# A channel-mixing stage whose two partition halves hold odd and even image rows instead of the same rows

## The chip, the cores and the metric

The kernel runs on one core of a Trainium2 chip. The metric is the device time of one execution in microseconds (us). All data are float32. Five engines work side by side and meet at semaphores: TensorE (PE in the profile; its weight loads are PEld), VectorE (DVE), ScalarE (ACT), GpSimd (POOL) and SyncE (SP), which only issues DMAs here. ScalarE and GpSimd issue DMAs too. A name such as ACTq or SPq is the engine's sequencer.

## The reference

The input x is 8 images x 64 channels x 256 x 256 pixels. Two layers are applied; only the first is touched by the change:

```python
x = x + _L0_conv_ref(_gn(x), ...)      # layer 0: the stage of this document
x = x + _L1_conv_ref(_gn(x), ...)      # layer 1: FFT, 32x32 modes mixed, inverse FFT
# inside _L0_conv_ref
y  = einsum('bwhc,dc->bwhd', xp, mlp1_w) + mlp1_b
x1 = _shift1(y[..., :c]);  x2 = _shift2(y[..., c:2*c])   # quarter of the channels each: one pixel
x3 = sigmoid(xn * wbn) * x                               # up, down, left, right, edges repeated
out = bar[:, 0] * x1 + bar[:, 1] * x2
o = (einsum('bwhc,dc->bwhd', out, mlp2_w) + mlp2_b) * x3
```

Since the shifts, the two products with matrices and the factors of `bar` are linear, an output pixel of layer 0 is a sum over four neighbours (above, below, left, right) of a 64x64 matrix by the 64 channels of that neighbour, plus a constant, times a gate `sigmoid(...)`, plus 1, times the centred input pixel.

## The kernel before

The program runs in stages, each ended by a barrier of all engines: statistics of x (0 to about 338 us), a short serial computation of the matrices and scales (to about 388 us), **the mixing stage** (to about 1471 us), the second normalisation, the forward transforms, the mixing of modes, and the inverse transforms. The change touches the end of the serial computation and the mixing stage.

The mixing stage handles 128 tiles: 8 images x 16 tiles of 16 image rows. They are numbered n = 0 to 31 in a body that runs 4 times (two images in each). There are 4 buffers of each kind (`mix_x`, `centred`, `gated`), 2 of `mix_out`, and two halves of PSUM. TensorE contracts over 128 partitions, twice the 64 channels, so two neighbours are summed in one pass. The lower 64 partitions hold an image row one column to the right of where the upper 64 hold it, and the upper ones hold the row one further down. Half of a tile's rows come by DMA into the lower partitions and half into the upper ones; VectorE copies each half to the other partitions. What each tile takes:

- SyncE (L565, L568): two loads of 9 rows x 64 channels, 576 KB each, when the tile four before has been convolved and gated.
- VectorE: copy `up` (L687) when both loads have landed; copy `down` (L692).
- GpSimd (L590, `pad`): two small products that repeat the edge columns, after `down`. They signal `padded`.
- TensorE (L618): 16 matrix products of 64 output channels x 512 pixels, after `padded`. A float32 product is two passes, so the trace has 32 records.
- ScalarE: centring of the pixel values (L641; two instructions of 64 partitions on even tiles, one on odd tiles, whose other half VectorE centres in L700), then the sigmoid (L649). It waits for `padded` too.
- VectorE: gate times convolution (L722, out of PSUM), later the output (L731).
- ScalarE: the store of the output (L662, 1024 KB), and the sum of its squares (L667).

The order on VectorE for tile n is: up(n+2), L722 of n, down(n+2), L731 of n, centre(n+2) if odd. On ScalarE: centring and sigmoid of n+2, store of n, square of n. Nothing reorders instructions within an engine.

The matrices stand in `wall`, 128 columns for each image: two slots of 64, for rows held in the lower and the upper partitions. At L503 32 instructions scale them out of PSUM. `take` (L677 to L679) fetches one image's matrices for the stage.

Of the kernel before, what the change touches and what calls it, by code (L numbers as in the profile page):

```python
# [23 lines left out]
ACT = mybir.ActivationFunctionType  # L24
ALU = mybir.AluOpType
# [19 lines left out]
LAYOUT = ((0, 0, 2), (1, 0, 1), (0, 1, 0), (1, 1, 3))  # L45
PITCH = W + 1
# [67 lines left out]
def program(nc, x, w1m, b1m, w2m, b2m, sa1, sa2, gamma, beta, wr1, wi1, wr2, wi2, const, out):  # L114
    top = ExitStack()
    with top:
# [34 lines left out]
        wall = sb(top, "wall", [P, B + 1, P])  # L151
# [7 lines left out]
        with ph:  # L159
# [133 lines left out]
            with nc.Block() as block:  # L293
# [77 lines left out]
                def _(dve):  # L371
# [141 lines left out]
        with ph:  # L513
            NX = 4
            XT = [sb(ph, f"mix_x{i}", [P, MR + 1, PITCH]) for i in range(NX)]
# [4 lines left out]
            one = sb(ph, "one", [P, MR + 1])  # L520
            wcur = [sb(ph, f"wcur{i}", [P, P]) for i in range(2)]
            pcur = [sb(ph, f"pcur{i}", [P, 6]) for i in range(2)]
            loaded = [sem(f"mix_loaded{i}") for i in range(NX)]
            stored = [sem(f"mix_stored{i}") for i in range(2)]
            one_set = sem("mix_one_set")
            doubled, padded, batch_ready = sem("mix_doubled"), sem("mix_padded"), sem("mix_batch_ready")
# [4 lines left out]
            ITER = B // 2  # L531

            x1_par = x1.rearrange("b (r e) c w -> b (e c) r w", e=2)

            def split(n):

                return n % 2 == 1

            def loaded_by(i, n):

                q, t = n % NX, n % NB
                edge = 16 if q in (0, NX - 1) else 0
                batch = NB // NX * 32 + edge
                return i * (2 * batch) + n // NB * batch + (t // NX + 1) * 32 + (edge if q == 0 or t == NB - 1 else 0)

# [6 lines left out]
            with nc.Block() as block:  # L552
                @block.sync
                def _(sp):
                    with sp.Fori(0, ITER) as i:
                        for n in range(NI):
                            ch = bass.ds((i * 2 + n // NB) * C, C)
                            t, xt = n % NB, XT[n % NX]


                            sp.wait_ge(conv_done, i * NI + n + 1)
                            sp.wait_ge(sig_done, i * NI + n + 1)
                            r0 = t * MR - 1
                            lo = max(r0, 0)
                            sp.dma_start(xt[0:C, lo - r0:MR // 2 + 1, 1:W + 1],  # L565
                                         x_rows[ch, lo:r0 + MR // 2 + 1, :]).then_inc(loaded[n % NX], 16)
                            hi = min(r0 + MR + 2, H)
                            sp.dma_start(xt[C:P, MR // 2:hi - r0 - 1, 0:W],  # L568
                                         x_rows[ch, r0 + 1 + MR // 2:hi, :]).then_inc(loaded[n % NX], 16)

                            if t == 0:
                                sp.dma_start(xt[0:C, 0:1, 1:W + 1], x_rows[ch, 0:1, :]).then_inc(loaded[n % NX], 16)
                            if t == NB - 1:
                                sp.dma_start(xt[C:P, MR:MR + 1, 0:W], x_rows[ch, H - 1:H, :]
                                             ).then_inc(loaded[n % NX], 16)

# [4 lines left out]
                def _(pool):  # L581
# [12 lines left out]
                    pad(0, 0)  # L594
                    pad(0, 1)

                    def body(i, final):
                        for n in range(NI - 2 * final):
                            pad(i, n + 2)

                    iterations(pool, body)

                @block.tensor
                def _(pe):
                    pe.sem_inc(conv_done, NX)
                    with pe.Fori(0, ITER) as i:
                        for n in range(NI):
                            j, k = n // NB, n % 2
# [13 lines left out]
                            last.then_inc(conv_done, 1)  # L622

                @block.scalar
                def _(act):
# [5 lines left out]
                    def gate(i, n):  # L631
# [7 lines left out]
                        for half in range(1 if split(n) else 2):  # L639
                            h = slice(half * C, (half + 1) * C)  # L640
                            last = nc.scalar.activation(  # L641
                                XC[n % NX][h, :].rearrange("p (r w) -> p r w", w=W),
# [710 lines left out]
```

## Time and profile before

| | us |
|---|---|
| device time, median of 3 runs (3144.79 to 3153.17) | 3149.35 |
| device time of the profiled execution | 3155.57 |
| span of the profiled execution | 3153.8 |
| mixing stage, first VectorE copy to last output | 397.2 to 1471.0 |
| VectorE busy in 430 to 1470 us | 966.1 of 1040 |
| TensorE busy there | 909.8 |
| ScalarE busy there | 865.6 |

The span runs from the first to the last instruction; the device time has 1.8 us more around it. Busy shares over the whole span (TensorE 71%, VectorE 64%) mix stages with different limits, so the mixing stage is read by itself. "Idle before" in the profile is the idle time of the engine just ahead of an instruction, with what ended it; "issue" means that nothing the profile shows was waited for. TensorE's granted clock was 0.96 of full speed in 430 to 1470 us.

### The profile page before, as it was taken

The page shows a single profiled execution, that of the slowest core. Times are in us where ns is not written, and L with a number is a line of the kernel's source. Part 1 is how long each engine was busy: PE and PEld are TensorE (multiplying, and loading weights), DVE is VectorE, ACT ScalarE, POOL GpSimd, SP SyncE. Part 2 cuts the span into 40 slices and gives each one's busy share as a digit, 9 for nine tenths or more (in the row PEclk, how much of TensorE's full clock was granted, in tenths as well). Part 3 has the DMA queues.
Part 4 walks back from the last instruction along what each step waited for, and adds up shares of the span by engine and source line. Part 5 has one row for each costly group of instructions (what it writes and reads, how often), then busy time and mean ns, then how long its engine had stood idle before and what let it go on. Part 6 is the DMA issues. An engine that isn't in the chain of part 4 may idle for free. (4 is left out here: it accounts for less than half of the span.)

```text
span 3153.8 us, 39097 instructions
## 1 busy us (share of the span) xinstructions
PE 2252.6 (71%) x12960; PEld 1081.7 (34%) x12960; DVE 2027.7 (64%) x2317; ACT 1298.2 (41%) x1470; POOL 756.3 (24%) x477
## 2 busy tenths in 40 slices
PE   0000289888989888885999999945554898988784
PEld 0000123223323232331455444425553444444442
DVE  8999689989999999996665565620000454544442
ACT  1111078878887888885332232310000222212220
POOL 1000022332233322332655455500000111111112
PEclk9999999999999999998999999977787999998987
DMA  9999199999999999997877666669998999999999
GB/s 400 429 429 429 36 248 265 271 248 275 270 272 256 270 274 270 269 267 233 316 261 266 241 242 247 232 145 295 304 305 231 384 401 380 394 380 408 389 378 351
DMA packets 537808, 942.87 MB, mean 299 GB/s; under 512 B 16896, under 2 KB 459952, under 8 KB 493136
## 3 DMA queue, kind: packets, MB, share of 16 engines
q1 hardware_dynamic: 299264, 613.33, 61.9%
q10 hardware_dynamic: 202880, 192.95, 20.1%
q0 software_dynamic: 35536, 134.84, 11.2%
q8 instruction: 85, 1.39, 0.2%
q14 instruction: 43, 0.35, 0.0%
HBM read 647.46 MB, written 293.60 MB: 298 GB/s over the span
## 5 line engine op out<-in xcount | busy, mean ns | idle before, releaser
L618 PE MATMUL psum<-mix_x,wcur 128*64 128x512 f32 x4096 | 937.6, 614 | 150.3 <-POOL mix_x L590 134.3
L618 PEld LDWEIGHTS psum<-mix_x,wcur 128*64 128x64 f32 x4096 | 316.6, 139 | 770.8 <-issue 566.4
L1259 PE MATMUL psum<-tab_irow_icol_sign,inv_t 128*128 128x512 f32 x1024 | 495.8, 608 | 18.9 <-DVE inv_x L1306 16.0
L590 POOL TENSOR_TENSOR mix_x<-mix_x,one 64x17 f32<-64x17 f32 x256 | 323.2, 1262 | 747.6 <-DVE mix_x L692 740.2
L641 ACT ACTIVATE centred<-mix_x,pcur 64x2048 f32<-64x2048 f32 x192 | 384.2, 2001 | 204.1 <-POOL mix_x L590 188.9
L1077 POOL TENSOR_TENSOR fwd_diff<-x_tile 128x2048 f32<-128x2048 f32 x64 | 307.9, 4812 | 291.7 <-PE psum L869 256.5
L983 ACT ACTIVATE fwd_rows<-psum 128x512 f32<-128x512 f32 x256 | 152.2, 597 | 412.8 <-PE psum L869 387.9
L263 DVE BATCH_NORM_STATS2 stats<-stat_x 128x512 f32 x512 | 310.0, 678 | 17.5 <-DMA stat_x<-x 14.7
L731 DVE SCALAR_TENSOR_TENSOR mix_out<-gated,centred 128x2048 f32<-128x2048 f32 x128 | 293.6, 2294 | 41.3 <-issue 35.5
L722 DVE SCALAR_TENSOR_TENSOR gated<-psum,pcur,gated 128x2048 f32<-128x2048 f32 x128 | 300.9, 2351 | 16.3 <-PE psum L618 14.4
L1052 DVE COPY fwd_cols<-psum 128x136 f32<-128x136 f32 x512 | 154.6, 394 | 234.2 <-PE psum L880 233.2
L869 PE MATMUL psum<-fwd_sum,tab_ident_frow_fcol 128*64 128x512 f32 x512 | 282.3, 635 | 30.1 <-POOL fwd_diff L1077 20.3
L1287 ACT ACTIVATE inv_t<-psum 128x256 f32<-128x256 f32 x256 | 98.1, 383 | 478.5 <-PE psum L1250 478.5
L1122 PE MATMUL psum<-mode_w,mode_x 128*16 128x64 f32 x4096 | 169.9, 360 | 162.5 <-DMA mode_x<-modes_in 159.8
L869 PE MATMUL psum<-fwd_diff,tab_ident_frow_fcol 128*64 128x512 f32 x512 | 282.7, 636 | 0.0
L649 ACT ACTIVATE gated<-centred,pcur 128x2048 f32<-128x2048 f32 x128 | 268.2, 2095 | 13.3 <-DVE centred L700 5.1
L1306 DVE TENSOR_TENSOR inv_x<-inv_x,psum 128x1024 f32<-128x1024 f32 x128 | 155.6, 1220 | 176.0 <-PE psum L1259 142.0
L1306 DVE TENSOR_TENSOR x_tile<-x_tile,psum 128x1024 f32<-128x1024 f32 x128 | 156.0, 1221 | 168.1 <-PE psum L1259 159.5
L1259 PEld LDWEIGHTS psum<-tab_irow_icol_sign,inv_t 128*128 128x128 f32 x1024 | 199.0, 196 | 167.6 <-issue 149.1
L297 PE MATMUL psum<-s_ones_dmask_spread_npix,w1d 128*64 128x128 f32 x1 | 0.4, 396 | 342.1 <-PEq L200 342.1
L667 ACT ACTIVATE square<-mix_out 128x2048 f32<-128x2048 f32 x128 | 242.5, 1894 | 3.6 <-DVE mix_out L731 3.6
L1250 PE MATMUL psum<-tab_irow_icol_sign,inv_yy 128*128 128x256 f32 x512 | 159.1, 395 | 100.6 <-ACT inv_yy L1281 100.6
(183 smaller groups left out, 1952.5 us busy)
## 6 DMA issues: line engine op xcount, KB each, us to landing
x_tile<-x_scratch SPq DMA_DIRECT2D x184, 1024.0 KB, 7.7
mix_x<-x SPq DMA_DIRECT2D x240, 576.0 KB, 8.2
stat_x<-x SPq DMA_DIRECT2D x64, 2048.0 KB, 14.4
x_scratch<-mix_out ACTq DMA_DIRECT2D x128, 1024.0 KB, 9.1
inv_x<-x_scratch SPq DMA_DIRECT2D x64, 1024.0 KB, 10.9
out<-x_tile POOLq DMA_DIRECT2D x64, 1024.0 KB, 17.0
out<-inv_x POOLq DMA_DIRECT2D x64, 1024.0 KB, 15.6
mode_w<-L_conv_w_imag ACTq DMA_DIRECT2D x16, 2048.0 KB, 21.2
```

The lines of the kernel that those rows point to most:

```text
L263: last = nc.vector.bn_stats(stats[:, bass.ds(b * (NT * 48) + (t * 8 + q) * 6, 6)], XT[t % NX][:, q * 512:(q + 1) * 512])
L590: last = nc.gpsimd.tensor_tensor(XT[n % NX][h, :, to], XT[n % NX][h, :, of], one[h, :], ALU.mult)
L618: last = nc.tensor.matmul(bank(k * 4 + q, 512, C, par * C), wcur[j][:, m * C:(m + 1) * C], XT[n % NX][:, r0:r0 + 3:2, m:m + W], start=(m = ...
L641: last = nc.scalar.activation(XC[n % NX][h, :].rearrange("p (r w) -> p r w", w=W), XT[n % NX][h, 1:MR:2, 1 - half:1 - half + W], ACT.Ident ...
L649: nc.scalar.activation(G[n % NX][:, :], XC[n % NX][:, :], ACT.Sigmoid, bias=pcur[j][:, 1:2], scale=pcur[j][:, 0:1]).then_inc(sig_done, 1)
L667: nc.scalar.activation(SQ[:, :], XO[k][:, :], ACT.Square, accum_out=sqs[:, bass.ds(i * NI + n, 1)]).then_inc(sq_done, 1)
L722: nc.vector.scalar_tensor_tensor(out=G[n % NX][:, :], in0=psum[:, k * SC:(k + 1) * SC], scalar=pcur[j][:, 3:4], in1=G[n % NX][:, :], op0=A ...
L731: nc.vector.scalar_tensor_tensor(out=XO[k][:, :], in0=G[n % NX][:, :], scalar=1.0, in1=XC[n % NX][:, :], op0=ALU.add, op1=ALU.mult, accum_ ...
L869: last = nc.tensor.matmul(bank(n % 2, 512, C, par * C), frow[:, par, :], ED[G0 % 2][par][:, 2 * cp:2 * cp + 2, :], start=True, stop=True)
L1077: nc.gpsimd.tensor_tensor(ED[G0 % 2][1][:, :, :], XW[G0 % NX][:, 0, :, :], XW[G0 % NX][:, 1, :, :], ALU.subtract).then_inc(diff_done, 1)
L1259: last = nc.tensor.matmul(bank(n % 2 * 2 + a), TS[n % 2][:, a * P:(a + 1) * P], icol, start=True, stop=True)
L1306: nc.vector.tensor_tensor(xw, xw, psum[:, n % 2 * 1024:n % 2 * 1024 + 1024] .rearrange("p (a k) -> p a k", a=2), ALU.add).then_inc(added, 1)
```

## The change

The two partition halves no longer hold the same rows. Odd image rows go to the lower 64 partitions, one column to the right, and even rows to the upper 64. A second set of buffers, `mix_a`, holds the same rows the other way aligned: VectorE copies each half within its own partitions. Of the 16 products of a tile the first eight (m = 0) read `mix_x` and the last eight (m = 1) read `mix_a`. Since neighbours swap their roles between even and odd output rows, there are four matrix slots of 64 columns for each image instead of two, and `LAYOUT` has eight entries; the scaling is one product per entry over all eight images.

Besides: the loads stay 9 rows x 64 channels each, but take every other row (1 KB each). Even rows are loaded from SyncE's queue, odd rows from ScalarE's, behind the store. `pad` waits for the loads alone, not for the copies, and has four products; ScalarE's centring waits for the loads alone; TensorE waits for `copied` only ahead of m = 1. VectorE centres in tiles 1 and 5 of every 8 instead of in every odd tile. `A_LOADED` is empty, so its branches add nothing.

```diff
-LAYOUT = ((0, 0, 2), (1, 0, 1), (0, 1, 0), (1, 1, 3))
-PITCH = W + 1
+LAYOUT = ((0, 0, 0), (1, 0, 3), (0, 1, 2), (1, 1, 1),
+          (0, 2, 1), (1, 2, 2), (0, 3, 3), (1, 3, 0))
...
-                    for b in range(B):
-                        for half, slot, d in LAYOUT:
-                            h = slice(half * C, (half + 1) * C)
-                            v.tensor_scalar(wall[h, b, slot * C:(slot + 1) * C], mats[h, b, d, :],
-                                            sm[h, 6, b:b + 1], None, ALU.mult)
+                    for half, slot, d in LAYOUT:
+                        h = slice(half * C, (half + 1) * C)
+                        v.tensor_tensor(wall[h, 0:B, slot * C:(slot + 1) * C], mats[h, :, d, :],
+                                        sm[h, 6, :].unsqueeze(2).to_broadcast([C, B, C]), ALU.mult)
...
-            XT = [sb(ph, f"mix_x{i}", [P, MR + 1, PITCH]) for i in range(NX)]
+            NK = TR // 2
+            XT = [sb(ph, f"mix_x{i}", [P, NK + 1, W + 2]) for i in range(NX)]
+            XA = [sb(ph, f"mix_a{i}", [P, NK, W + 1]) for i in range(NX)]
...
+            ODD, EVEN = slice(0, C), slice(C, P)
+            A_LOADED = ()
+            CENTRE_DVE = (1, 5)
...
+                            sp.wait_ge(conv_done, i * NI + n + 1)
+                            sp.wait_ge(sig_done, i * NI + n + 1)
+                            count = NK + (t != NB - 1)
+                            last = min(t * TR + 2 * NK, H - 2)
+                            sp.dma_start(xt[EVEN, 0:count, 0:W],
+                                         x_rows[ch, t * TR:last + 1:2, :]).then_inc(loaded[q], 16)
...
-                        pool.wait_ge(doubled, i * NI + n + 1)
-                        for half, to, of in ((0, 0, 1), (1, W, W - 1)):
-                            h = slice(half * C, (half + 1) * C)
-                            last = nc.gpsimd.tensor_tensor(XT[n % NX][h, :, to], XT[n % NX][h, :, of],
-                                                           one[h, :], ALU.mult)
+                        xt, xa = XT[n % NX], XA[n % NX]
+                        pool.wait_ge(loaded[n % NX], loaded_by(i, n))
...
+                        for h, to, of in ((ODD, xt[ODD, :, 0], xt[ODD, :, 1]),
+                                          (EVEN, xt[EVEN, :, W], xt[EVEN, :, W - 1]),
+                                          (ODD, xa[ODD, :, W], xt[ODD, 1:NK + 1, W]),
+                                          (EVEN, xa[EVEN, :, 0], xt[EVEN, 0:NK, 0])):
+                            last = nc.gpsimd.tensor_tensor(to, of, one[h, 0:to.shape[1]], ALU.mult)
                         last.then_inc(padded, 1)
...
                             for m in range(2):
-                                for q in range(4):
+                                if m == 1 and not a_by_dma(n):
+                                    pe.wait_ge(copied, i * len(COPIES) + copies_before(n) + 1)
+                                for q in range(NK // 2):
                                     for par in range(2):
-                                        r0 = 1 - m + par + q * 4
+                                        if m == 0:
+                                            src = xt[:, 2 * q + par:2 * q + par + 2, 1 - par:1 - par + W]
+                                        else:
+                                            src = xa[:, 2 * q:2 * q + 2, par:par + W]
                                         last = nc.tensor.matmul(bank(k * 4 + q, 512, C, par * C),
-                                                                wcur[j][:, m * C:(m + 1) * C],
-                                                                XT[n % NX][:, r0:r0 + 3:2, m:m + W],
-                                                                start=(m == 0), stop=(m == 1))
+                                                                wcur[j][:, (2 * m + par) * C:(2 * m + par + 1) * C],
+                                                                src, start=(m == 0), stop=(m == 1))
...
-                        act.wait_ge(padded, i * NI + n + 1)
+                        act.wait_ge(loaded[n % NX], loaded_by(i, n))
...
+                    def load_odd(i, n):
...
+                        act.dma_start(xt[ODD, int(t == 0):NK + 1, 1:W + 1],
+                                      x_rows[ch, r0:t * TR + TR:2, :]).then_inc(loaded[q], 16)
...
+                    for n in range(NX):
+                        load_odd(0, n)
...
+                            if not (final and n + NX >= NI):
+                                act.wait_ge(conv_done, i * NI + n + NX + 1)
+                                act.wait_ge(sig_done, i * NI + n + NX + 1)
+                                load_odd(i + (n + NX) // NI, (n + NX) % NI)
...
+                    def first(i, n):
 
                         dve.wait_ge(loaded[n % NX], loaded_by(i, n))
...
+                        if not a_by_dma(n):
+                            nc.vector.tensor_copy(XA[n % NX][ODD, :, 0:W], XT[n % NX][ODD, 1:NK + 1, 1:W + 1])
+
+                    def second(n):
+
+                        if not a_by_dma(n):
+                            nc.vector.tensor_copy(XA[n % NX][EVEN, :, 1:W + 1], XT[n % NX][EVEN, 0:NK, 0:W]
+                                                  ).then_inc(copied, 1)
```

On ScalarE, from the start of the repeated body, the store of tile n (`x_scratch<-mix_out`) stood between the sigmoid of n+2 and the square of n. Before:

```order
L641 ACTIVATE centred<-mix_x,pcur 64x2048 x2
L649 ACTIVATE gated<-centred,pcur 128x2048
L661 REGISTER_ALU
L662 ISA
L662 DMA x_scratch<-mix_out 128x8x256
L666 REGISTER_ALU
L667 ISA
L667 ACTIVATE square,sqs<-mix_out 128x2048
L636 REGISTER_ALU
L641 ACTIVATE centred<-mix_x,pcur 64x2048
```

The same place in the changed kernel:

```order
L680 ACTIVATE centred<-mix_x,pcur 64x2048 x2
L686 ACTIVATE gated<-centred,pcur 128x2048
L710 REGISTER_ALU
L711 ISA
L711 DMA x_scratch<-mix_out 128x8x256
L694 ISA
L694 DMA mix_x<-x 64x9x256
L720 REGISTER_ALU
L721 ISA
L721 ACTIVATE square,sqs<-mix_out 128x2048
L675 ISA
L677 REGISTER_ALU
```

The load of the odd rows (L694, for tile n+4) now stands behind the store on ScalarE and its queue, ahead of the square; the next tile's centring has two instructions there, where it had one.

On VectorE, one tile after the first of the body. Before (L687 is `up`, L692 `down`, L700 the centring of the tile two on):

```order
L687 COPY mix_x<-mix_x 64x8x256
L720 REGISTER_ALU
L722 SCALAR_TENSOR_TENSOR gated<-psum,pcur,gated 128x2048
L692 COPY mix_x<-mix_x 64x8x256
L728 REGISTER_ALU
L730 REGISTER_ALU
L731 ISA
L731 SCALAR_TENSOR_TENSOR mix_out,sums<-gated,centred 128x2048
L700 TENSOR_SCALAR centred<-mix_x,pcur 64x2048
L685 REGISTER_ALU
```

In the changed kernel the same tile:

```order
L745 COPY mix_a<-mix_x 64x8x256
L768 REGISTER_ALU
L770 SCALAR_TENSOR_TENSOR gated<-psum,pcur,gated 128x2048
L750 COPY mix_a<-mix_x 64x8x256
L776 REGISTER_ALU
L778 REGISTER_ALU
L779 ISA
L779 SCALAR_TENSOR_TENSOR mix_out,sums<-gated,centred 128x2048
L739 REGISTER_ALU
```

The two copies stay where they were, and the centring behind the output is gone from this tile.

## Rows read from the trace of the kernel before

**Rows 1.** Windows: width, busy us (count) of PE PEld DVE ACT POOL, clock, DMA, GB/s.

```profile
core 0: us, PE busy (x) PEld busy (x) DVE busy (x) ACT busy (x) POOL busy (x), PEclk, DMA share, GB/s
100.00:300.00 200.00, 0.00 (x0) 0.00 (x0) 197.90 (x327) 30.98 (x174) 0.00 (x0) 1.00 1.01 428
393.00:408.00 15.00, 7.60 (x26) 2.42 (x28) 6.24 (x5) 7.52 (x5) 1.79 (x4) 0.60 1.13 202
430.00:1470.00 1040.00, 909.80 (x3982) 307.57 (x3978) 966.12 (x709) 865.55 (x563) 314.22 (x248) 0.96 1.04 266
1014.70:1016.20 1.50, 1.50 (x8) 0.41 (x6) 1.49 (x2) 1.39 (x2) 0.00 (x0) 1.00 1.09 386
1018.00:1021.50 3.50, 3.14 (x16) 0.85 (x12) 3.35 (x6) 2.13 (x4) 2.56 (x2) 1.00 1.12 205
```

**Rows 2.** Waits, 430 to 1470 us: who <- for whom: us, times, longest.

```profile
POOL mix_x L590 <- DVE mix_x L692: 712.1, 124, 17.0
ACT centred L641 <- POOL mix_x L590: 143.9, 59, 10.6
PE psum L618 <- POOL mix_x L590: 110.4, 72, 5.7
DVE mix_out L731 <- issue: 35.5, 41, 2.0
DVE gated L722 <- PE psum L618: 14.4, 11, 4.8
```

**Rows 3.** Groups by line, 430 to 1470 us: count, busy us, mean ns, idle before.

```profile
L641 ACT ACTIVATE centred<-mix_x,pcur 64x2048 f32<-64x2048 f32 x186 | 372.2, 2001 | 159.1 <-POOL mix_x L590 143.9 <-issue 14.4
L590 POOL TENSOR_TENSOR mix_x<-mix_x,one 64x17 f32<-64x17 f32 x248 | 314.2, 1267 | 719.3 <-DVE mix_x L692 712.1
L722 DVE SCALAR_TENSOR_TENSOR gated<-psum,pcur,gated 128x2048 f32<-128x2048 f32 x125 | 293.9, 2351 | 16.2 <-PE psum L618 14.4
L731 DVE SCALAR_TENSOR_TENSOR mix_out<-gated,centred 128x2048 f32<-128x2048 f32 x126 | 289.0, 2294 | 41.2 <-issue 35.5 <-DMA x_scratch<-mix_out 3.1
L649 ACT ACTIVATE gated<-centred,pcur 128x2048 f32<-128x2048 f32 x125 | 261.9, 2095 | 13.2 <-DVE centred L700 5.1 <-ACT centred L641 0.8
L692 DVE COPY mix_x<-mix_x 64x2048 f32<-64x2048 f32 x124 | 151.8, 1224 | 3.9
L700 DVE TENSOR_SCALAR centred<-mix_x,pcur 64x2048 f32<-64x2048 f32 x62 | 79.8, 1287 | 2.0
```

**Rows 4.** DMA issues: count, KB each, us to landing; 430:1470, then 388:400 us.

```profile
mix_x<-x SPq DMA_DIRECT2D x227, 576.0 KB, 8.1
x_scratch<-mix_out ACTq DMA_DIRECT2D x125, 1024.0 KB, 9.1
...
mix_x<-x SPq DMA_DIRECT2D x1, 512.0 KB, 5.4
```

**Rows 5.** DMA queues, 1024.5 to 1026 us: packets, MB, share of 16 engines.

```profile
q1 hardware_dynamic: 261, 0.27, 55.5%
q10 hardware_dynamic: 295, 0.29, 55.3%
```

**Rows 6.** Timeline, 1007 to 1028 us: start, us, what [idle before].

```profile
1007.54 0.60 SPq L568 DMA_DIRECT2D mix_x<-x  x1
...
1009.37 0.38 ACTq L662 DMA_DIRECT2D x_scratch<-mix_out  x1
...
1014.03 7.11 PE L618 MATMUL psum<-mix_x,wcur 128*64 128x512 f32 x32 [0.56 <-POOL mix_x L590]
...
1026.42 0.51 POOL L590 TENSOR_TENSOR mix_x<-mix_x,one 64x17 f32<-64x17 f32 x2 [4.97 <-DVE mix_x L692]
...
1027.34 2.29 DVE L731 SCALAR_TENSOR_TENSOR mix_out<-gated,centred 128x2048 f32<-128x2048 f32 x1 [1.00 <-issue]
```

**Rows 7.** Timeline of the serial computation before the stage, 366 to 388 us.

```profile
366.93 0.69 DVE L487 TENSOR_TENSOR w2s<-psum,w2t 128x512 f32<-128x512 f32 x1
...
378.37 9.52 DVE L503 TENSOR_SCALAR wall<-psum,sm 64x64 f32<-64x64 f32 x32 [6.82 <-PE psum L353]
```

More of the change, by code:

```diff
@@ L150, in program @@
         params = sb(top, "params", [P, B + 1, 4])
-        wall = sb(top, "wall", [P, B + 1, P])
+        wall = sb(top, "wall", [P, B + 1, 4 * C])
         sums = sb(top, "sums", [P, B * NT])
@@ L519, in program @@
             SQ = sb(ph, "square", [P, SC])
-            one = sb(ph, "one", [P, MR + 1])
-            wcur = [sb(ph, f"wcur{i}", [P, P]) for i in range(2)]
+            one = sb(ph, "one", [P, NK + 1])
+            wcur = [sb(ph, f"wcur{i}", [P, 4 * C]) for i in range(2)]
             pcur = [sb(ph, f"pcur{i}", [P, 6]) for i in range(2)]
             loaded = [sem(f"mix_loaded{i}") for i in range(NX)]
+            a_loaded = [sem(f"mix_a_loaded{i}") for i in range(NX)]
             stored = [sem(f"mix_stored{i}") for i in range(2)]
             one_set = sem("mix_one_set")
-            doubled, padded, batch_ready = sem("mix_doubled"), sem("mix_padded"), sem("mix_batch_ready")
+            copied, padded, batch_ready = sem("mix_copied"), sem("mix_padded"), sem("mix_batch_ready")
             xc_done, sig_done, conv_done, sq_done = (sem("mix_" + n) for n in ("xc", "sig", "conv", "sq"))
@@ L531, in program, with a_by_dma, centre_dve, copies_before @@
             ITER = B // 2
-            x1_par = x1.rearrange("b (r e) c w -> b (e c) r w", e=2)
-            def split(n):
-                return n % 2 == 1
+            ODD, EVEN = slice(0, C), slice(C, P)
+            A_LOADED = ()
+            CENTRE_DVE = (1, 5)
+            COPIES = [n for n in range(NI) if n % 8 not in A_LOADED]
+            CENTRES = [n for n in range(NI) if n % 8 in CENTRE_DVE]
+            x1_par = x1.rearrange("b (r e) c w -> b (e c) r w", e=2)
+            def a_by_dma(n):
+                return n % 8 in A_LOADED
+            def centre_dve(n):
+                return n % 8 in CENTRE_DVE
+            def copies_before(n):
+                return sum(m < n for m in COPIES)
+            def centres_before(n):
+                return sum(m < n for m in CENTRES)
             def loaded_by(i, n):
@@ L544, in loaded_by, with a_loaded_by, row_pair @@
                 return i * (2 * batch) + n // NB * batch + (t // NX + 1) * 32 + (edge if q == 0 or t == NB - 1 else 0)
+            def a_loaded_by(i, n):
+                mine = [m for m in range(NI) if a_by_dma(m) and m % NX == n % NX]
+                return i * (len(mine) * NK * 16) + (mine.index(n) + 1) * NK * 16
+            def row_pair(first, step):
+                return bass.AP(x.tensor, first, [[C * NPIX, B], [step, 2], [NPIX, C], [1, W + 1]])
             def iterations(engine, body):
@@ L554, in _, with load @@
                 def _(sp):
+                    def load(i, n):
+                            bs = bass.ds(i * 2 + n // NB, 1) if not isinstance(i, int) else slice(i * 2 + n // NB, i * 2 + n // NB + 1)
+                            ch = bass.ds((i * 2 + n // NB) * C, C) if not isinstance(i, int) else slice((i * 2 + n // NB) * C, (i * 2 + n // NB + 1) * C)
+                            t, xt, xa, q = n % NB, XT[n % NX], XA[n % NX], n % NX
+                            sp.wait_ge(conv_done, i * NI + n + 1)
[4 more added lines that the diff above has]
+                                         x_rows[ch, t * TR:last + 1:2, :]).then_inc(loaded[q], 16)
+                            if t == NB - 1:
+                                sp.dma_start(xt[EVEN, NK, 0:W], x_rows[ch, H - 1, :]).then_inc(loaded[q], 16)
+                            if a_by_dma(n):
+                                for k in range(NK):
+                                    sp.dma_start(xa[:, k, :],
+                                                 row_pair((t * TR + 2 * k + 1) * W, -W - 1)[bs][0]
+                                                 ).then_inc(a_loaded[q], 16)
@@ L555, in _ @@
                     with sp.Fori(0, ITER) as i:
                         for n in range(NI):
[L557 to L575, printed above, removed]
+                            load(i, n)
@@ L585, in pad @@
                     def pad(i, n):
[L587 to L601 removed]
+                        xt, xa = XT[n % NX], XA[n % NX]
+                        pool.wait_ge(loaded[n % NX], loaded_by(i, n))
+                        if a_by_dma(n):
+                            pool.wait_ge(a_loaded[n % NX], a_loaded_by(i, n))
+                        for h, to, of in ((ODD, xt[ODD, :, 0], xt[ODD, :, 1]),
[3 more added lines that the diff above has]
+                            last = nc.gpsimd.tensor_tensor(to, of, one[h, 0:to.shape[1]], ALU.mult)
+                        last.then_inc(padded, 1)
+                    with pool.Fori(0, ITER) as i:
+                        for n in range(NI):
+                            pad(i, n)
                 @block.tensor
@@ L708, in _ @@
                     for n in range(2):
-                        up(0, n)
-                        down(n)
-                    centre(0, 1)
+                        first(0, n)
+                        second(n)
                     def body(i, final):
@@ L717, in body @@
                             if ahead:
-                                up(i, n + 2)
+                                first(i, n + 2)
                             dve.wait_ge(conv_done, i * NI + NX + n + 1)
@@ L725, in body @@
                             if ahead:
-                                down(n + 2)
+                                second(n + 2)
                             dve.wait_ge(h_done, i * NI + 2 + n + 1)
@@ L735, in body @@
                                                            ).then_inc(o_done, 1)
-                            if ahead and split(n + 2):
-                                centre(i, n + 2)
                             if n % NB == NB // 2:
```

41 lines of the change are left out of this document (20 added, 21 removed).

## The prediction, made before the changed kernel was run

> **What bounds the kernel now.** I read the windows first, then the waits, the groups by line, and the DMA views, all of the mixing stage. In 430 to 1470 us VectorE has 125 instructions of L722, one for each tile, so a tile takes 1040/125 = 8.32 us. Per tile VectorE is busy 966.1/125 = 7.73 us, TensorE 7.28, ScalarE 6.92 [rows 1, 3]. VectorE is the nearest to a bound, with 0.59 us of idle time a tile. The waits say where it comes from: 35.5 us ahead of L731 for nothing that the profile names, 14.4 us for TensorE [rows 2]; the remaining 24 us are short gaps, 0.19 us a tile. The 35.5 us belong to GpSimd: in the timeline the pair of pads runs from 1026.42 for 0.51 us, and L731, which should follow the copy, starts at 1027.34 after 1.00 us idle [rows 6]. When the pads lose that race they take long instead: 1.27 us each on average, over 0.25 in the pair shown [rows 3, 6]. TensorE and ScalarE wait for the pads, 110 and 144 us [rows 2]: pads wait for the copy `down`, which stands behind L722 of two tiles before. So VectorE, GpSimd and TensorE form a ring in which nobody runs ahead.
>
> The DMA engines are the second bound. Per tile they carry two loads of 576 KB and a store of 1024 KB, 2.23 MB, which at 8.32 us is 268 GB/s, as the window has it (266). When loads alone run they make 202 to 205 GB/s; a store alone makes 386, and the statistics stage, whose loads fill all 128 partitions, 428 [rows 1]. So a load into 64 partitions goes at half rate. One after the other a tile's transfers would take 1.18/0.203 = 5.8 us and 1.05/0.386 = 2.7, together 8.5 us, more than the tile. They fit only because a store and a load overlap at their ends: in 1.5 us queue q10 (stores) moved 0.29 MB and q1 (loads) 0.27, 180 GB/s for the load as if it were alone [rows 5]. No engine waits for it, though; only the latency of a load would show.
>
> **The change part by part.**
>
> *Matrices.* 32 scalings at L503 take 9.52 us in a row; now 8 products of 64x512 out of PSUM. The nearest row is the 128x512 product out of PSUM, 0.69 us [rows 7]. 8 x 0.69 = 5.5, a gain of 4.0 us on a serial path. Bounds: 0.4 each (gain 6) and 1.0 each (gain 1.5).
>
> *VectorE.* Copies stay, 64x2048 at 1.22 us each. The centring falls from 1 in 2 tiles to 1 in 4: 0.25 x 1.29 = 0.32 us a tile less. Busy 7.73 - 0.32 = 7.41, with short gaps 0.19 it is 7.60. The L722 waits for TensorE (0.12 a tile) go, see below. `take` copies 256 columns instead of 128, once in 16 tiles: nothing.
>
> *Pads.* Four instead of two, 9 and 8 elements instead of 17, started by the loads and not by the copy. By the mean of 1.27 us they take 5.1 us a tile instead of 2.5, between 1.0 (0.25 each, unhindered) and 9.5 (2.4 each, one VectorE instruction each); below the tile's time but for the last. VectorE pays now 0.28 us a tile for the race (35.5/125). It could be 0 if the pads fall under L722, or 1.0 if every tile loses as the one shown. I keep 0.28, as the row has it: 7.60 + 0.28 = 7.88.
>
> *ScalarE.* 0.25 x 2.00 = 0.50 more a tile, 6.92 + 0.50 = 7.42, and it no longer waits for the pads. It issues the load of odd rows, 0.60 us as SyncE does, behind the store's 0.38 [rows 6]. Behind these waits the square; the sigmoid (2.10 us) runs meanwhile and hides both if the output is done by then. Uncovered they cost up to 1.0, which makes 8.4; I take 0.2 and 7.6.
>
> *TensorE.* The same 16 products, 7.11 us [rows 6]. They start on the pads, which no longer hang on L722. Tile n+1 can start when L722 of n-1 has read its half of PSUM, and `copied` comes 1.2 us after that, well ahead of m = 1. TensorE gets ahead by most of a tile. This takes the 110 us of waits off the ring.
>
> *Loads.* Same bytes (9 + 9 rows before and after), every other row. Even rows for n+5 are issued about 1.4 us into L722 of n (2.35 + 7.11 less one tile); nobody needs them for a tile and a half. Odd rows for n+4 are issued only when the output of n is done. VectorE needs them at `first` of n+4, right behind the output of n+1. That closes a new ring over two tiles: output done, signal and store issue 0.58; the load's latency L; then first 1.22 and its share of centring 0.32, L722 2.35, second 1.22, output 2.37, gaps 0.2. Twice the tile's time is at least 8.25 + L. For L: the first load of the stage landed 5.4 us after its issue with 512 KB [rows 4], of which 2.6 is data at 202 GB/s, so 2.8 are fixed. Behind the store: 2.8 + 2.7 (store) + 2.9 (own data) - 0.5 (store issued earlier) = 7.9 us. The ring then is (8.25 + 7.9)/2 = 8.08 us. Bounds of L: 5.0 if the even rows and the store cost it nothing, 10.3 if the even load of n+6, whose data starts 0.5 us into it, takes half the engines and adds the remaining 2.4.
>
> *A rule against it.* The Trainium skill (SBUF — State Buffer, "Can I just issue two DMAs to hit both halves?") says that two DMAs at once, one at partition 0 and one at 64, came out only 6% faster than one: they serialise. The windows of loads, 202 and 205 GB/s, agree for two DMAs of one queue; rows 5 shows a load and a store of two queues side by side, 371 GB/s. By the rule a tile's transfers would stay at 5.5 + 2.7 = 8.2 us, by the row they could fall to about 5.8.
>
> *Sum.* VectorE with the pads gives 7.88, the load ring 8.08, ScalarE 7.6. I take 8.10, at which the DMA moves 275 GB/s. (8.32 - 8.10) x 128 = 28 us. Matrices 4.0. The start of the stage: the loads of the first tiles ran at 202 GB/s; on two queues they may land earlier, by 0 to 5 us; I take 1. The profiled execution took 3155.6: 3155.6 - 33 = 3122.6. It stood 6.2 above the median of the runs, so 3116 us.
>
> **The rivals.**
>
> *B, both halves load side by side.* If odd and even rows on two queues use different sides of the memory, the loads of a tile cost nearly the time of one. L falls towards 6 and VectorE with its pads binds: 7.88, and 7.8 if it wins the race more often. (8.32 - 7.85) x 128 = 60, with 4 and 4 for the start: 3149 - 68 = 3081. For: rows 5. Against: 202 GB/s for pairs of loads, and the rule above.
>
> *C, the freed time is taken back.* Twice as many pads, now started while VectorE is anywhere, cost it 0.7 us a tile instead of 0.28: 7.60 + 0.7 = 8.3, and only the matrices are gained: 3145. For: each of the 41 waits cost 0.87 us (35.5/41). Against: under L722 no wait of VectorE shows.
>
> *D, slower: the odd rows come late.* One mechanism: the odd load waits behind the 1 MB store, and shares the engines with the next even load. VectorE then waits at `first` (L739) in each tile. It decides from L = 2 x 8.32 - 8.25 = 8.4 us, 0.5 above my estimate. With L = 9.1 the tile is 8.68 and the kernel takes 3149 + 46 - 5 = 3190; with 10.3 it is 9.28: +123 - 5 = 3267. For: stores land after 9.1 us at the median now, and this load stands behind one [rows 4]. Against: the store's 9.1 contains the two loads issued just ahead of it (the second at 1007.54, the store at 1009.37 [rows 6]); now the even load is issued some 5 us earlier. The Trainium skill (DMA: Bandwidth & Descriptors, "Queues, rings and completion order") has each DMA engine take turns between queues, which is what would slow the odd load; rows 5 shows such turns, without a loss for the load.
>
> **How the numbers follow.** Forecast 0.42, its own range 3098 to 3138; B 0.18; C 0.14; D 0.26. Likeliest 3116. The range for 8 in 10 is 3070 to 3200: it takes in B and C, and the part of D up to L = 9.3, about half of it; outside are 0.13 of D and 0.03 below. 0.3% of 3149 is 9.4 us, about what the measurement can tell from no change. Faster: forecast and B, 0.60. Same: C, 0.14. Slower: D, 0.26.
>
> **What would show it.** The scaling of the matrices near 5.5 us. In the stage: TensorE without waits for pads but with waits for L770; ScalarE busy about 7.4 us a tile; the centring on VectorE at 32 instructions. The ring of loads right: VectorE waits a little for `mix_x<-x` at L745 or L742, odd loads land after some 8 us. B: loads above 300 GB/s while no store runs, and no waits for DMA. C: idle time ahead of L779, L745 or L750 for "issue". D: long waits of VectorE for DMA, odd loads landing after more than 8.5 us. The prediction is wrong in its core if the tile takes under 7.85 or over 8.4 us, or if ScalarE turns out to be what the others wait for.

## The result, and the profile after

The changed kernel takes 3206.4 us (median of 4 runs, 3202.35 to 3217.43); the kernel before 3151.3 beside it. The ratio is 1.017, 95% interval 1.015 to 1.019: slower by 1.7%, clear of the noise. The forecast was 3116. The profiled execution took 3217.4 us, 61.8 over that of before. From the first load to the last output the mixing stage went from 1082.4 to 1145.5 us, +63.1; the matrices gave 4.0 back; what follows the stage took 2.7 more. So the whole loss lies in the stage. L770 to L770 a tile takes 8.90 us on the mean of tiles 8 to 120; for before the same count gives 8.35.

The stage's window for the changed kernel, columns as in [rows 1]:

```profile
430.00:1520.00 1090.00, 912.49 (x3934) 329.43 (x3932) 902.30 (x669) 924.47 (x583) 274.46 (x491) 0.95 1.04 250
```

VectorE was busy 93% of the stage before, now 83% (902.3 of 1090). ScalarE is at 85%. The DMA moves 250 GB/s instead of 266. No engine is at a bound. That is the picture of a ring: a circle of waits in which each step needs the one before it, so the time round it decides, not the work of one engine. The waits of the changed kernel in this stretch, as in [rows 2]:

```profile
POOL mix_x L624 <- DMA mix_x<-x: 789.8, 122, 10.0
PE psum L651 <- DVE gated L770: 160.5, 79, 5.8
ACT square L721 <- issue: 131.9, 36, 5.8
DVE mix_a L745 <- DMA mix_x<-x: 106.8, 63, 4.5
DVE centred L742 <- DMA mix_x<-x: 73.2, 31, 5.0
```

VectorE now waits 180 us for loads, at the first thing that it does for a tile; in [rows 2] there was no such wait. TensorE no longer waits for the pads but for VectorE to free PSUM. ScalarE's 131.9 us "issue" ahead of the square are, by the order of its program, its wait for the output, with store and load issued behind it. The waits in [rows 2] ahead of L731, 35.5 us, are gone: L779 now has 3.8.

```profile
L680 ACT ACTIVATE centred<-mix_x,pcur 64x2048 f32<-64x2048 f32 x215 | 430.2, 2001 | 17.0 <-issue 11.4 <-DMA mix_x<-x 1.4
L770 DVE SCALAR_TENSOR_TENSOR gated<-psum,pcur,gated 128x2048 f32<-128x2048 f32 x123 | 287.2, 2335 | 0.0
L779 DVE SCALAR_TENSOR_TENSOR mix_out<-gated,centred 128x2048 f32<-128x2048 f32 x123 | 282.1, 2293 | 3.8
L624 POOL TENSOR_TENSOR mix_x<-mix_x,one 64x9 f32<-64x9 f32 x245 | 188.4, 769 | 797.0 <-DMA mix_x<-x 789.8
```

The instructions last what they lasted in [rows 3], but the pads are shorter: 0.77 us here and 0.35 for the two on `mix_a`, not 1.27. The DMA view, as in [rows 4]:

```profile
x_scratch<-mix_out ACTq DMA_DIRECT2D x122, 1024.0 KB, 6.5
mix_x<-x ACTq DMA_DIRECT2D x115, 576.0 KB, 8.8
mix_x<-x SPq DMA_DIRECT2D x112, 576.0 KB, 8.3
```

And two tiles in the timeline, start and duration, with the idle time before:

```profile
1000.46 2.29 DVE L779 SCALAR_TENSOR_TENSOR mix_out<-gated,centred 128x2048 f32<-128x2048 f32 x1
...
1003.03 2.10 ACT L686 ACTIVATE gated<-centred,pcur 128x2048 f32<-128x2048 f32 x1
1003.25 0.39 ACTq L711 DMA_DIRECT2D x_scratch<-mix_out  x1
1003.86 0.62 ACTq L694 DMA_DIRECT2D mix_x<-x  x1
...
1013.64 1.22 DVE L745 COPY mix_a<-mix_x 64x2048 f32<-64x2048 f32 x1
1013.69 1.51 POOL L624 TENSOR_TENSOR mix_x<-mix_x,one 64x9 f32<-64x9 f32 x2 [5.65 <-DMA mix_x<-x]
...
1018.41 2.29 DVE L779 SCALAR_TENSOR_TENSOR mix_out<-gated,centred 128x2048 f32<-128x2048 f32 x1
```

The output of a tile ends at 1002.75. ScalarE is still centring for another tile, dispatches its sigmoid at 1003.03, and issues store and odd load at 1003.25 and 1003.86. The load lands 9.8 us later, at 1013.62, and the copy of that tile starts at 1013.64. The output that follows two tiles on ends at 1020.7: 18 us for two tiles.

### The profile page after: what moved, and what is told of

It is laid out like the page before. It is cut to its first block and busy times, and to the rows that moved or that the text cites. A ratio compares the mean times of both kernels' runs of the same rounds, so it can differ in the third digit from the quotient of the medians.

```text
span 3215.5 us, 39423 instructions
## 1 busy us (share of the span) xinstructions
PE 2271.3 (71%) x12960; PEld 1108.6 (34%) x12960; DVE 1971.2 (61%) x2261; ACT 1374.5 (43%) x1502; POOL 719.1 (22%) x733
## 5 line engine op out<-in xcount | busy, mean ns | idle before, releaser
L651 PE MATMUL psum<-mix_x,wcur 128*64 128x512 f32 x2048 | 516.5, 645 | 194.9 <-DVE gated L770 160.5
L651 PE MATMUL psum<-mix_a,wcur 128*64 128x512 f32 x2048 | 471.4, 596 | 0.0
L680 ACT ACTIVATE centred<-mix_x,pcur 64x2048 f32<-64x2048 f32 x224 | 448.2, 2001 | 48.1 <-DMA mix_x<-x 32.4
L624 POOL TENSOR_TENSOR mix_x<-mix_x,one 64x9 f32<-64x9 f32 x256 | 194.5, 760 | 830.9 <-DMA mix_x<-x 823.4
L651 PEld LDWEIGHTS psum<-mix_x,wcur 128*64 128x64 f32 x2048 | 171.7, 146 | 528.4 <-issue 510.3
L721 ACT ACTIVATE square<-mix_out 128x2048 f32<-128x2048 f32 x128 | 243.5, 1903 | 149.6 <-issue 131.9
L770 DVE SCALAR_TENSOR_TENSOR gated<-psum,pcur,gated 128x2048 f32<-128x2048 f32 x128 | 299.0, 2336 | 1.9 <-PE psum L651 1.9
L779 DVE SCALAR_TENSOR_TENSOR mix_out<-gated,centred 128x2048 f32<-128x2048 f32 x128 | 293.5, 2293 | 4.0
L651 PEld LDWEIGHTS psum<-mix_a,wcur 128*64 128x64 f32 x2048 | 171.9, 137 | 275.4 <-issue 274.8
```

The costliest lines, as they stand in the source:

```text
L624: last = nc.gpsimd.tensor_tensor(to, of, one[h, 0:to.shape[1]], ALU.mult)
L651: last = nc.tensor.matmul(bank(k * 4 + q, 512, C, par * C), wcur[j][:, (2 * m + par) * C:(2 * m + par + 1) * C], src, start=(m == 0), stop ...
L680: last = nc.scalar.activation(out, rows, ACT.Identity, bias=pcur[j][(EVEN, ODD)[half], 4:5])
L721: nc.scalar.activation(SQ[:, :], XO[k][:, :], ACT.Square, accum_out=sqs[:, bass.ds(i * NI + n, 1)]).then_inc(sq_done, 1)
L770: nc.vector.scalar_tensor_tensor(out=G[n % NX][:, :], in0=psum[:, k * SC:(k + 1) * SC], scalar=pcur[j][:, 3:4], in1=G[n % NX][:, :], op0=A ...
L779: nc.vector.scalar_tensor_tensor(out=XO[k][:, :], in0=G[n % NX][:, :], scalar=1.0, in1=XC[n % NX][:, :], op0=ALU.add, op1=ALU.mult, accum_ ...
```

## The experiments

The ring theory: the odd load for tile n+4 leaves after the output of n and its store, and VectorE needs it right behind the output of n+1. Its work from there ends with the output of n+2, two tiles after the start of the circle. So two tiles cannot take less than the way round. Rival S: ScalarE has too much work, since it centres in three tiles of four. Rival R: every other row loads more slowly. The runs were made in three groups, e1 to e4, e5 to e8, e9 and e10, each with runs of the kernel before beside it; where times of different groups are subtracted below, the ratios to the kernel before give the same within 7 us.

For each kernel the way round was read from the trace (means of tiles 8 to 119, us). The four parts always add up to two tiles, so the sum alone shows no ring; the ring binds where the third, from landing to the copy, is small. It holds a few hundredths for the signal and VectorE's centring, 1.3 us in one tile of four. In the changed kernel VectorE starts on a tile within 0.15 us of the landing in 85 of 112 tiles, in e2 in 60, in e3 in 72, in e1 in none.

| kernel | output done to issue | issue to landing | landing to first copy | first copy to output n+2 | tile |
|---|---|---|---|---|---|
| before (upper load) | -7.29 | 9.28 | 7.06 | 7.65 | 8.35 |
| changed | 1.09 | 8.94 | 0.64 | 7.14 | 8.90 |
| e1, all on SyncE | -9.47 | 10.30 | 7.02 | 7.34 | 7.60 |
| e2, odd load before output | 0.47 | 7.23 | 0.78 | 7.14 | 7.81 |
| e3, load ahead of store | 1.31 | 6.75 | 0.64 | 7.15 | 7.92 |
| e4, before, split queues | 4.73 | 8.36 | 0.08 | 7.25 | 10.21 |
| e5, centring in odd tiles | 0.95 | 8.67 | 0.87 | 7.14 | 8.82 |
| e10, first copy later | 1.28 | 9.73 | 0.89 | 4.86 | 8.38 |

**e1: all loads on SyncE.**

```diff
 # SyncE, behind the even rows of the same tile
+                            sp.dma_start(xt[ODD, int(t == 0):NK + 1, 1:W + 1],
+                                         x_rows[ch, r0:t * TR + TR:2, :]).then_inc(loaded[q], 16)
 # ScalarE
-                    for n in range(NX):
-                        load_odd(0, n)
...
-                                load_odd(i + (n + NX) // NI, (n + NX) % NI)
```

> The changed kernel with one edit: the odd rows are loaded by SyncE right behind the even rows of the same tile (both when the tile four before is convolved and gated), and ScalarE issues only stores. Ring theory (the odd load is issued only after the output of tile n, behind the store, and VectorE needs it at the output of n+1): the ring is gone, VectorE no longer waits for mix_x<-x, a tile takes 8.0 to 8.2 us instead of 8.90, and the kernel 3095 to 3130 us, faster than before. Rival S (ScalarE has too much work since it centres in three tiles of four, and TensorE and VectorE follow it): a tile stays over 8.5 us, 3165 us or more, and the idle time of VectorE moves to a wait for ScalarE. Rival R (rows read every other one are slower to load): loads alone run under 190 GB/s and VectorE still waits for them, 3180 or more.

Measured: 3058.3 us, ratio to before 0.970 (0.967 to 0.972). That is 148 us under the changed kernel. VectorE waits for no load any more. Window and waits of this kernel:

```profile
430.00:1370.00 940.00, 873.18 (x3950) 320.20 (x3946) 902.05 (x673) 923.62 (x588) 182.74 (x488) 0.99 1.08 292
```

```profile
PE psum L656 <- DVE gated L768: 49.5, 40, 2.8
DVE mix_out L777 <- issue: 21.4, 25, 2.4
```

Direction and mechanism are as the ring theory had it, but the gain is larger than expected: 7.60 us a tile, not 8.0 to 8.2, and 3058 us, not 3095 to 3130. ScalarE is busy 98% here, VectorE 96%. Rivals S and R fall as causes of the slowdown: ScalarE does the same centring and the rows are the same ones.

**e2: odd load on ScalarE, ahead of the wait for the output.** The block with `load_odd` moves up, with its own waits (left out here):

```diff
+                                load_odd(i + (n + NX) // NI, (n + NX) % NI)
                             act.wait_ge(o_done, i * NI + NX + n + 1)
                             act.dma_start(x1_par[...], XO[k]...)
```

> The changed kernel with the odd load still on ScalarE's queue, but issued ahead of the wait for the output of tile n, so ahead of that tile's store too. Ring theory: the load leaves 3 to 6 us earlier and has no store ahead of it, VectorE stops waiting for it, 8.0 to 8.2 us a tile, within 10 us of the kernel with all loads on SyncE. Rival S: no gain, 3165 or more. If only the sharing of the DMA engines by two queues delayed the load, it would still land late, after 8.5 us, and the gain would be under half.

Measured: 3077.5 us, 0.976 (0.974 to 0.979), 7.81 us a tile: 19 us over e1, where at most 10 were expected, and faster than the 8.0 to 8.2 us a tile named. The detail was a miss too. The load still leaves 0.47 us after the output on the mean, not 3 to 6 us earlier, since ScalarE is then just done with the centring of n+2; only the store is out of its way, and VectorE still waits for loads, 44 us in all:

```profile
DVE centred L742 <- DMA mix_x<-x: 23.1, 29, 1.5
DVE mix_a L745 <- DMA mix_x<-x: 21.0, 29, 2.0
```

The two queues are still there, and 129 of the 148 us are back. So it is not two queues in themselves that cost the time.

**e3: the load ahead of the store, both after the output.**

```diff
                             act.wait_ge(o_done, i * NI + NX + n + 1)
+                                load_odd(i + (n + NX) // NI, (n + NX) % NI)
                             act.dma_start(x1_par[...], XO[k]...)
```

> The changed kernel with the order of the two DMAs on ScalarE swapped: after the output of tile n first the odd load of n+4, then the store of n. Ring theory with the store's 2.7 us of data as part of the latency: the load's latency falls from 8.9 to about 6.2 us and its issue comes 0.6 earlier, the ring asks only for (17.8 - 3.3)/2 = 7.3 us and no longer binds; 8.0 to 8.3 us a tile, 3100 to 3145. If the latency is not the store's, but that of the even load sharing the engines, it stays near 8 and the tile near 8.5 us, 3155 or more.

Measured: 3092.6 us, 0.981 (0.979 to 0.984). The latency falls from 8.94 to 6.75 us, by 2.2 us. The time is 7 us under the range named (3100 to 3145), and 7.92 us a tile is under its 8.0 to 8.3. The argument was too kind all the same: the latency is not 6.2, the issue after the output is not earlier (1.31), and the ring still binds in most tiles, with 52 us of VectorE's waits (28.8 at L744, 23.1 at L741).

**e4: the queue part alone, in the kernel before.**

```diff
-                            sp.dma_start(xt[C:P, MR // 2:hi - r0 - 1, 0:W],
+                        act.dma_start(xt[C:P, MR // 2:hi - r0 - 1, 0:W],   # behind the store of tile n
                                       x_rows[ch, r0 + 1 + MR // 2:hi, :]).then_inc(loaded[n % NX], 16)
```

> The kernel before with the queue part of the change alone: the load of the upper partitions goes from SyncE to ScalarE, behind the store of tile n. Ring theory: the same ring arises, and it is longer, since here the store is issued 4.2 us after the output (ScalarE waits for the pads): 4.9 + 8.9 + 7.6 = 21.4 us for two tiles, 10.7 a tile at most, and if ScalarE gets ahead in the slower kernel down to 8.9; 3220 to 3450 us, clearly slower than before, with VectorE waiting for mix_x<-x. If two queues in themselves cost nothing and the loss came from the layout or ScalarE's load, it stays within 10 us of before.

Measured: 3385.8 us, 1.074 (1.071 to 1.077). Its waits in 430 to 1370 us:

```profile
PE psum L610 <- POOL mix_x L582: 221.3, 86, 6.0
DVE mix_x L698 <- DMA mix_x<-x: 218.7, 91, 5.7
```

Without any of the new layout the moved load makes the kernel before 7% slower, 10.2 us a tile, inside the range named. VectorE starts on the load when it lands (0.08 in the table). Queue and position of the load are enough for a loss.

**e5: the changed kernel with VectorE centring in every odd tile.** `CENTRE_DVE = (1, 3, 5, 7)`.

> The changed kernel, loads as they are (odd rows on ScalarE behind the store), with VectorE centring half of every odd tile as before (tiles 1, 3, 5, 7 of eight): ScalarE has 0.5 us a tile less, VectorE 0.32 more. Ring theory: the ring stays; its terms change by -0.4 (ScalarE is free sooner to issue) and +0.3 to +0.6 over two tiles (centring ahead of the copy), so 8.8 to 9.0 us a tile and 3190 to 3220 us. Rival S (ScalarE's load made the changed kernel slow): a tile falls to 8.4 us or less, 3150 us or less.

Measured: 3204.0 us, 1.018 (1.015 to 1.020); the changed kernel had 1.017. With 0.5 us a tile taken from ScalarE and 0.32 given to VectorE nothing moves. Rival S is out.

**e6: the same with all loads on SyncE.**

> All loads on SyncE, and VectorE centring half of every odd tile as before. With the ring gone the two engines' own work decides: VectorE busy 7.22 + 0.32 = 7.54 us a tile, with the idle time of 0.38 it had, 7.8 to 7.95; ScalarE 6.9. 3080 to 3105 us, 20 to 45 us over the kernel with all loads on SyncE and tiles 1 and 5. If nothing but ScalarE bounds that kernel (busy 98%), the tile would get shorter instead, under 7.5 us.

Measured: 3073.8 us, 0.976 (0.974 to 0.977), 7.78 us a tile. Here the engines' own work counts: VectorE is busy 921.4 of 940 us. The tile comes out just under the range named, the time just under it too. The fewer centrings are worth 15 us, and only once the ring is gone.

**e7: all loads on SyncE, pads and centring waiting as before the change.**

```diff
-                        pool.wait_ge(loaded[n % NX], loaded_by(i, n))
+                        pool.wait_ge(copied, i * NI + n + 1)
...
-                        act.wait_ge(loaded[n % NX], loaded_by(i, n))
+                        act.wait_ge(padded, i * NI + n + 1)
```

> All loads on SyncE, but the waits as before the change: the pads wait for the second copy, and ScalarE's centring waits for the pads. If the gain of the kernel with all loads on SyncE comes from the cut ring of copies, pads and TensorE, it goes: TensorE and ScalarE wait for the pads again by 0.8 to 1.1 us a tile, 8.1 to 8.5 us a tile, 3120 to 3165 us. If it comes from the fewer centrings on VectorE alone, the tile stays within 0.1 us of 7.60.

Measured: 3153.8 us, 1.001 (1.000 to 1.003), 8.38 us a tile, in the range named: the whole gain is gone, though VectorE has less to do than before and the matrices are 4 us cheaper. Its waits, in 430 to 1370 us:

```profile
PE psum L656 <- POOL mix_a L629: 99.3, 53, 6.0
ACT centred L685 <- POOL mix_a L629: 85.7, 47, 8.6
DVE mix_out L777 <- issue: 53.2, 54, 3.4
DVE gated L768 <- PE psum L656: 41.4, 25, 6.3
```

These are the waits of [rows 2] again.

**e9: of the two, the pads alone wait for the copy.**

> All loads on SyncE; the pads alone wait for the second copy again, ScalarE's centring waits for the loads. It splits what the version with both late waits lost (7.60 to 8.37 us a tile). If the loss comes over the pads to TensorE and over their collision with VectorE's L777, nearly all of it stays: 8.1 to 8.4 us a tile, 3120 to 3155 us. If it comes from ScalarE, which starts its 7.4 us of work late, the kernel stays near 7.7 us a tile, 3065 to 3080 us.

Measured: 3087.7 us, 0.980 (0.975 to 0.986), 7.91 us a tile; between the two expectations. The late pads cost 29 us; ScalarE's late start on top of them costs 66 more (e7 less e9). Neither theory alone was right: ScalarE, with 7.4 us of work in a tile, cannot afford to wait for the pads.

```profile
PE psum L656 <- POOL mix_a L629: 75.4, 102, 2.2
DVE gated L768 <- PE psum L656: 50.5, 76, 7.3
```

**e10: the changed kernel, load unmoved, VectorE's need for it later.**

```diff
-                            if ahead:
-                                first(i, n + 2)
 # L770 of tile n
                             if ahead:
+                                first(i, n + 2)
                                 second(n + 2)
```

> The changed kernel with the odd load where it is, behind the store on ScalarE, but VectorE's wait for it and the first copy of tile n+2 moved behind L770 of tile n. It leaves the load's issue and latency alone and takes L770 (2.34 us) out of the two-tile ring: 1.09 + 8.9 + 0.64 + 7.14 - 2.34 = 15.5 us, 7.7 us a tile. Ring theory: 7.7 to 8.0 us a tile, 3070 to 3110 us, though the load is as late as ever. If the slow part is the load or ScalarE in itself (less DMA throughput, an in-order queue that is too full), the tile stays over 8.5 us, 3170 us or more.

Measured: 3141.8 us, 0.999 (0.996 to 1.001): 65 us better than the changed kernel with the load left alone, but 8.38 us a tile and not the 7.7 to 8.0 expected. The last part of the ring fell by 2.28 as planned; the latency rose from 8.94 to 9.73, and TensorE now waits for pads:

```profile
PE psum L651 <- POOL mix_a L624: 97.2, 54, 3.5
DVE mix_a L745 <- DMA mix_x<-x: 41.8, 49, 1.9
```

The latency is no constant of the ring. In the trace the even loads' queue moved 762 KB on the mean between an odd load's issue and its landing, in the changed kernel 598 KB. The 164 KB more take 0.8 us at the 205 GB/s of loads in one queue, which is the rise; that is an estimate, and no run tried it by itself.

**e8: meant as the fastest.** e1 with `CENTRE_DVE = (1, 4, 6)`.

> A version meant to be the fastest: all loads on SyncE, VectorE centring in three tiles of eight (1, 4, 6). ScalarE 7.39 - 0.25 = 7.14 us busy a tile, VectorE 7.22 + 0.16 = 7.38: the larger of the two is 0.01 under what it was, with idle time 7.5 to 7.65 us a tile, 3040 to 3065 us.

Measured: 3054.9 us, 0.969 (0.968 to 0.971), 7.61 us a tile. It beats both kernels, and is level with e1 (0.970, intervals overlap). In 430 to 1370 us VectorE is busy 922 of 940 and ScalarE 898: work has moved from one to the other, and VectorE, 98% busy, is now the nearest to a bound.

## Why the prediction was wrong

The prediction named a tile over 8.4 us as the sign that its core was wrong, and the tile takes 8.90. Its likeliest case failed in one step: "The ring then is (8.25 + 7.9)/2 = 8.08 us". The ring itself was right, place and order; it is rival D, given 0.26, and it decides. Two of its terms were too small, and they make the sum:

- **The latency.** Taken as 7.9, measured 8.94. The 7.9 had the load behind the store and nothing else in the way; the bound upwards, 10.3, had most of an even load in it. In the trace of the changed kernel an even load is in flight when the store is issued in 108 of 112 tiles, and another even load is issued before the odd one lands in 109. Between the odd load's issue and its landing the even loads' queue moved 598 KB on the mean, about one whole load. For the load issued at 1003.86, the queues in 1006.5 to 1009 us, then in 1009.5 to 1013.5 us (packets, MB, share of 16 engines; q1 has the even loads, q10 the stores and odd loads):

```profile
q10 hardware_dynamic: 928, 0.94, 106.0%
q1 hardware_dynamic: 8, 0.01, 2.3%
...
q1 hardware_dynamic: 451, 0.46, 62.5%
q10 hardware_dynamic: 368, 0.36, 49.6%
```

  First the store runs alone. Then the odd load shares the engines with the next even one, at 204 GB/s for both together. So what the term left out are the even loads: its 2.9 us for the load's own data hold only with nothing beside it. What the store ahead costs is at most the 2.2 us of e3: there the even loads' queue moved 518 KB in the time of an odd load, 80 less, so not all of the 2.2 is the store.
- **The rest of the way round.** Taken as 8.25 us, measured 1.09 + 0.64 + 7.14 = 8.87. From the output to the issue of the load 0.58 had been allowed, and 1.09 are measured. In the middle tile it is 0.80 from the end of L779 (the table counts 0.07 less): the store is issued 0.18 after the output, the load 0.6 behind the store. The mean is higher because ScalarE comes late in 40 of 112 tiles, since the centring and sigmoid of n+2 stand ahead of the wait, and by over 7 us in the two tiles with which the repeated body starts anew. In ScalarE's own sum 0.2 us were put down for such delays and none in the ring. VectorE's own part, from the copy to the output, was taken as 7.36 and is 7.14. The 0.64 holds 0.33 of centring, as allowed, and the slack of the 27 tiles in which the load had landed in time.

Together 1.04 + 0.62 = 1.66 us in two tiles, 0.83 a tile, times 128 tiles 106 us: the forecast 3116 becomes 3222, beside 3206 measured. The latency alone would have made (8.25 + 8.94)/2 = 8.60 us a tile and 3180 us, inside the range of 3070 to 3200; it took both terms to leave it. The point from which D decides, 8.4 us of latency, held only for the small terms; with the measured ones it is 2 x 8.35 - 8.87 = 7.8.

What else was right or wrong:

- *Matrices.* Forecast 8 x 0.69 = 5.5 us, measured:

```profile
378.30 5.60 DVE L502 TENSOR_TENSOR wall<-psum,sm 64x512 f32<-64x512 f32 x8 [6.84 <-PE psum L353]
```

- *TensorE's waits for pads go.* Right, and worth more than thought: e7 against e1 shows 95 us for the waits of pads and centring, where the sum of all gains in the stage had been 28.
- *VectorE's floor.* Put at 7.88 us with the race against the pads kept at 0.28. In e1 it waits 21.4/125 = 0.17 there and a tile takes 7.60. The pads take less than the 1.27 us of the row they were sized by: in e1 the two kinds take 0.51 and 0.24 us. The prediction had named 0.25 as the unhindered time, and that this is what lengthens them beside VectorE was not tried by itself.
- *The DMA as second bound.* Not where it was put. The transfers of a tile, one after the other, were reckoned at 8.5 us, and the 8.10 us stood at 275 GB/s; e1 runs the stage at 292 GB/s with all loads in one queue.
- *Rival B, loads side by side.* Seen at the start of the stage, not in it. While the first loads of the stage run and no store does, the changed kernel moves 291 GB/s, e1 and the kernel before 206 and 203. Windows of the three, in this order:

```profile
388.00:402.00 14.00, 6.31 (x16) 1.86 (x18) 6.25 (x5) 9.14 (x5) 6.34 (x8) 0.52 1.10 291
```

```profile
388.00:402.00 14.00, 6.49 (x18) 1.95 (x20) 6.19 (x5) 9.32 (x5) 6.21 (x8) 0.54 1.13 206
```

```profile
392.00:406.00 14.00, 5.60 (x16) 1.75 (x18) 5.40 (x5) 5.52 (x4) 0.86 (x4) 0.53 1.13 203
```

  In seven of these us both queues had loads, and there the rate is over the 300 GB/s that the prediction asked for. The changed kernel and e1:

```profile
394.00:401.00 7.00, 5.31 (x14) 1.61 (x16) 4.75 (x5) 6.93 (x5) 4.81 (x7) 0.50 1.09 346
```

```profile
394.00:401.00 7.00, 5.49 (x14) 1.67 (x16) 3.83 (x4) 6.93 (x5) 3.92 (x6) 0.51 1.13 205
```

  The rule cited from the Trainium skill (SBUF — State Buffer, "Can I just issue two DMAs to hit both halves?") gives 6% for two DMAs at once; at the start of the stage two queues gave 41% over 14 us and 69% in the seven, so there the measurement decides. Later in the stage the trace agrees with the rule: an even load is issued some 5 us before the odd one, so for the most part they run one after the other, and in the half microseconds in which an odd load and the even loads' queue each moved over a quarter of the packets, both together made 209 GB/s (median of 122). Why the rates added up at the start and not there is not shown. L did not fall towards 6.
- *Rival C* did not occur: VectorE's waits for the pads fell.

## What to carry to other kernels

Moving a DMA to another engine's queue moves it in that engine's order too: ask which wait it now stands behind, and write the way round to its user, with the work that the issuing engine has ahead of it. A load whose buffer is long free should be issued by an engine that has nothing else to wait for. And read the parts of a change apart: here one part (pads and centring on the loads alone) was worth 95 us and another (the moved load) cost 148, and the sum looked like a small loss. A latency read in one place is not a constant either: it grows with what other queues have in flight, 6.75 to 9.73 us for the same load in these runs.

## What the runs showed of the hardware

- Loads into the lower and the upper 64 partitions on two queues, with nothing else running, moved 346 GB/s over 7 us, against 205 on one queue. Between stores, later in the same stage, the same pair of queues made 209.
- A load of 576 KB behind a store of 1 MB on the same queue lands 2.2 us later than ahead of it (8.94 and 6.75 us). Of the 8.94 us a good part goes with the other queue, which moves 598 KB in that time.
- The small GpSimd products have no fixed duration: two on 17 elements took 0.51 us in one place and 3.6 in others, and the mean was 1.27 us each where they started with the copies' end; in e1 those on 9 and 8 elements took 0.51 and 0.24 us. Their busy time says little of their work.
